# Fewer transposes between the products of an expert pair, another split of the work between engines, and another placing of the shared blocks in a gated attention and mixture-of-experts layer

## What is computed

```python
n = layernorm(x)
q, k, v = n @ W_q, ctx @ W_k, ctx @ W_v             # 8 heads of 64
attn = softmax(where(mask, q @ k.T / 8, -max))      # 1024 x 154 per head and sequence
x = x + tanh(g_xattn) * (attn @ v @ W_o + b_o)
n = layernorm(x)
scores = sigmoid(n @ gate_w.T)                      # 32 experts in 8 groups
idx = top 6 of (scores + e_bias) in the best 4 groups
w = scores[idx] / sum(scores[idx]) * 2.5
moe = sum over the 6 of w * (relu(n @ up[e].T) ** 2 @ down[e].T)       # inner width 128
shared = relu(n @ shared_up.T) ** 2 @ shared_down.T                    # inner width 512
x = x + tanh(g_ffn) * (moe + shared)
```

## Time and profile before

| | us |
|---|---|
| median of 3 runs | 822.31 (818.47 to 823.46) |
| profiled execution | 824.46 |
| its span, first to last instruction | 822.7 |
| TensorE busy in the span | 757.1 |
| GpSimd busy | 502.9 |
| VectorE busy | 447.8 |
| ScalarE busy | 389.8 |
| mean granted clock of TensorE | 0.981 |

### The profile page before, as it was taken

The page is one execution under the profiler, slowest core; times in us unless marked ns, Lnnn a source line. Parts: engine busy times, 40 slices in busy tenths (PEclk is TensorE's granted clock), DMA queues, the critical chain, the costliest instruction groups (busy, mean ns, idle before and its releaser), DMA issues.

```text
span 822.7 us, 17866 instructions
## 1 busy us (share of the span) xinstructions
PE 757.1 (92%) x5833; PEld 639.1 (78%) x5833; DVE 447.8 (54%) x1591; ACT 389.8 (47%) x1141; POOL 502.9 (61%) x471
## 2 busy tenths in 40 slices
PE   3998989999999999979999999999999999999954
PEld 2986878888888888866656678889999887888943
DVE  0426445667666666663562124444444587766775
ACT  1126555565666665652542325555545554454520
POOL 2803221248787878787777715767767777776760
PEclk9999999999999999999999999999999999999986
DMA  8900000015221212342838446666667999999988
GB/s 284 346 10 1 1 2 1 2 37 181 76 90 71 91 71 91 115 147 100 316 115 292 149 126 180 200 207 196 206 202 218 313 370 363 332 327 298 314 303 293
DMA packets 77612, 144.72 MB, mean 176 GB/s; under 512 B 12625, under 2 KB 58961, under 8 KB 77009
## 3 DMA queue, kind: packets, MB, share of 16 engines
q1 hardware_dynamic: 51936, 63.89, 25.5%
q0 software_dynamic: 19968, 56.52, 18.3%
q10 hardware_dynamic: 5616, 23.16, 8.4%
HBM read 73.80 MB, written 69.73 MB: 174 GB/s over the span
## 4 chain that ended last, share of the span: by engine, by line
PE 61%; POOL 15%; ACT 8%; issue 6%; DMA 4%; DVE 4%; DVEq 1%; POOLq 0%; SPq 0%
POOL token_parts L409 15%; PE ps L1086 7%; PE ps L982 6%; PE ps L1138 6%; PE ps L1265 5%; PE ps L1029 5%; PE ps L1150 5%; PE ps L1282 5%; PE ps L1064 4%; PE ps L1001 4%; ACT att L460 3%; PE ps L1251 3%; ACT att L469 2%; PE ps L1076 2%; DMA token_parts<-hid,place 2%
## 5 line engine op out<-in xcount | busy, mean ns | idle before, releaser
L409 POOL DMA_INDIRECT token_parts<-hid,place x224 | 223.2, 996 | 99.1 <-issue 64.3
L392 POOL DMA_INDIRECT routed_rows<-x_n,slots x120 | 117.0, 975 | 34.3 <-issue 34.3
L1265 PE MATMUL ps<-big,att 128*128 x896 | 121.5, 279 | 3.9 <-issue 2.6
L1265 PEld LDWEIGHTS ps<-big,att 128*128 128x128 f32 x896 | 110.2, 193 | 10.3 <-issue 9.7
L1282 PE MATMUL ps<-big,att 128*128 x448 | 115.7, 381 | 0.6 <-ACT att L552 0.6
L548 ACT ACTIVATE att<-ps 128x512 f32<-128x512 f32 x112 | 66.9, 597 | 90.1 <-PE ps L1251 90.1
L385 POOL TENSOR_TENSOR att<-att,rsum 128x1232 f32<-128x1232 f32 x22 | 49.4, 2245 | 87.8 <-DVE rsum L666 87.6
L469 ACT ACTIVATE att<-ps 128x512 f32<-128x512 f32 (+1 forms) x96 | 47.0, 525 | 115.9 <-PE ps L1064 115.9
L1282 PEld LDWEIGHTS ps<-big,att 128*128 128x128 f32 x448 | 76.8, 192 | 6.6 <-issue 0.8
L911 DVE TENSOR_SCALAR att<-ps 128x256 f32<-128x256 f32 x112 | 47.6, 425 | 58.5 <-PE ps L1265 55.1
L552 ACT ACTIVATE att<-ps 128x256 f32<-128x256 f32 x112 | 42.9, 383 | 62.6 <-PE ps L1273 62.6
(11 more groups left out here) (221 smaller groups left out, 1333.5 us busy)
## 6 DMA issues: line engine op xcount, KB each, us to landing
mid<-routed_rows SPq DMA_DIRECT2D x224, 138.0 KB
big<-token_parts ACTq DMA_DIRECT2D x19, 768.0 KB, 7.1
x_n<-token_parts ACTq DMA_DIRECT2D x9, 768.0 KB
routed_rows<-pad_row SPq DMA_DIRECT2D x1, 4416.0 KB, 21.3
routed_rows<-pad_row SPq DMA_DIRECT2D x32, 138.0 KB, 2.9
big<-in_x SPq DMA_DIRECT2D x4, 1024.0 KB, 14.6
big<-in_w_moe SPq DMA_DIRECT2D x2, 2048.0 KB, 8.9
big<-in_w_moe SPq DMA_DIRECT2D x1, 4096.0 KB, 13.8
```

What stands on the lines that cost most here:

```text
L392: nc.gpsimd.indirect_dma_start(rows, bass.IndirectOffsetOnAxis(ap=slots[:, t, k:k + 1], axis=0), normed(t), None).then_inc(s_sca[t // TB % ...
L409: nc.gpsimd.indirect_dma_start(parts, bass.IndirectOffsetOnAxis(ap=place[:, p // 2 % 4, p % 2 * 2 + j:p % 2 * 2 + j + 1], axis=0), y_sb[:, ...
L1265: ins = M(ps[:, 2 + p % 2, j * P:(j + 1) * P], xt[:, p % 2, j * 256 + c * P:j * 256 + (c + 1) * P], w_exp[:, bass.ds(e, 1), c * P:(c + 1) ...
```

## The change

There are six parts.

- **Pairs on TensorE.** `expert_up` has the weights as the stationary operand and the transposed rows as the moving one, so its output is already transposed and `hidden_t` is gone. The weights are copied ahead of that, by ScalarE, from the register-addressed place to one of two fixed buffers (`copy_up`). VectorE makes relu and square in two instructions (`relu_square`). `rows_t` runs two pairs ahead instead of one.
- **Output buffers.** `y_sb` has eight buffers instead of four.
- **Scaling.** Of the tiles T = 11 to 31 those with T % 4 equal to 3 or 0 (eleven) are scaled by VectorE, behind the maxima of the next tile. GpSimd sends six scatters in each iteration from T = 12 on.
- **Shared blocks.** `GAP` is 5. Blocks 5 and 6 are done between the pairs, in 16 steps at pairs 4, 10, ..., 94, and block 7 behind the last pair. The first two blocks' `down` is cut in halves around the router's products of the last block.
- **Nine token groups** instead of four, ending at tiles 4, 8, 12, 16, 20, 24, 28, 30 and 32. The table has 288 rows in three pieces, and its products are 2 columns wide where only one is used. A group's number of pairs `DONE` is 3t + 16 for an end at tile t.
- **Parts.** Tiles 0 to 23 are loaded one in three pairs from pair 32 on (32, 35, 38, 41, 44, ... 101), tiles 24 to 27 at 104, 106, 108 and 110. Of the last four, 28 and 29 wait only for the pairs of the group that ends at tile 30.

```diff
-GAP = 7
-NSEG = 4
+GAP = 5
+DVE_NORM = tuple(t for t in range(11, NT) if t % 4 in (3, 0))
-SEG_END = (12, 20, 28, NT)
+SEG_END = (4, 8, 12, 16, 20, 24, 28, 30, NT)
+PART_LOAD = {DONE[g] + 4 + 3 * i: 4 * g + i for g in range(6) for i in range(4)}
+PART_LOAD.update({DONE[6] + 4 + 2 * i: 24 + i for i in range(4)})
-SHARED_STEP = {2 + 6 * i: i for i in range(8 * (NBLK - GAP))}
+SHARED_STEP = {4 + 6 * i: i for i in range(8 * (NBLK - 1 - GAP))}
...
@@ gpsimd
                 if T >= 12:
-                    for i in range(sent, sent + 5 + T % 2):
+                    for i in range(sent, sent + TOPK):
                         scatter(i)
-                    sent += 5 + T % 2
-                normalise(T)
+                    sent += TOPK
+                if T not in DVE_NORM:
+                    normalise(T)
...
@@ scalar
-            def square(p):
-                act.wait_ge(s_ehp, p + 1)
-                A.activation(h_t[:, p % 2, :], ps[:, 2 + p % 2, 256:512], ACT.Square).then_inc(s_eht, 1)
+            def copy_up(p):
+                if p == 0:
+                    act.wait_ge(s_row, 1)
+                    for i in range(3):
+                        act.wait_ge(s_we[i], 16)
+                if p % 2 == 0:
+                    act.load(regs[p // 2 % 2], exp_i[0:1, 2 * p:2 * p + 4])
+                for j in range(2):
+                    e = act.snap(regs[p // 2 % 2][p % 2 * 2 + j], min_val=0, max_val=NE - 1)
+                    ins = A.activation(w_up[p % 2][:, j, :], w_exp[:, bass.ds(e, 1), 0:256].rearrange("p a n -> p (a n)"), ACT.Copy)
+                ins.then_inc(s_ewu, 1)
...
@@ vector
+            def normalise(T):
+                p3 = prob[T % 3][:, 0:HJ].rearrange("p (h j) -> p h j", h=NH)
+                V.tensor_tensor(p3, p3, rsum[:, T % 2, :].unsqueeze(2).broadcast_to([P, NH, J]), ALU.mult).then_inc(s_pnv, 1)
...
                     for q in range(3):
                         maxima(T, q)
+                if T - 1 in DVE_NORM:
+                    dve.drain()
+                    normalise(T - 1)
...
-                        dve.wait_ge(s_ys[p % 4], 32 * ((p - 8) // 4 + 1))
+                        dve.wait_ge(s_ys[p % 8], 32 * (p // 8))
...
-            def relu(p):
+            def relu_square(p):
                 dve.wait_ge(s_eup, p + 1)
-                V.tensor_scalar(h_tok[:, p % 2, :], ps[:, 2 + p % 2, 0:256], 0.0, None, ALU.max).then_inc(s_ere, 1)
+                h, r = ps[:, 2 + p % 2, 0:256], relu[p % 2]
+                V.tensor_scalar(r, h, 0.0, None, ALU.max)
+                dve.drain()
+                V.scalar_tensor_tensor(h_t[:, p % 2, :], h, 0.0, r, ALU.max, ALU.mult).then_inc(s_eht, 1)
...
@@ tensor
             def expert_up(p):
+                pe.wait_ge(s_xts, p + 1)
+                pe.wait_ge(s_ewu, p + 1)
+                for j in range(2):
+                    for c in range(KC):
+                        ins = M(ps[:, 2 + p % 2, j * P:(j + 1) * P], w_up[p % 2][:, j, c * P:(c + 1) * P],
+                                xt[:, p % 2, j * 256 + c * P:j * 256 + (c + 1) * P],
+                                start=c == 0, stop=c == KC - 1, skip_group_check=True)
+                ins.then_inc(s_eup, 1)
...
-                if p + 1 < N_PAIRS:
-                    rows_t(p + 1)
+                if p + 2 < N_PAIRS:
+                    rows_t(p + 2)
                 if p >= 1:
                     expert_down(p - 1)
-                if p < N_PAIRS:
-                    hidden_t(p)
```

261 lines of the change are left out of this document (153 added, 108 removed).

## The result

The changed kernel took 788.75 us (median of 4 runs, 786.80 to 789.22), the kernel before 821.36 (median of 4, 818.47 to 823.46) on the same chip: ratio 0.9596, 95% interval 0.9565 to 0.9628. The forecast was 788, range 774 to 806. Medians and ranges, here and in the experiments, are over all executions of a kernel, while ratios leave out the ones over 1.5% above its fastest. The changed kernel's profiled execution has a span of 787.4 us against 822.7.

What follows compares the result with a forecast made beforehand. TensorE was taken to bound attention, shared blocks and the pairs up to 617 us, then GpSimd's scatters, held up by VectorE's additions. Start 474 + pairs 293 + tail 21 = 788 us, range 774 to 806.

Steps and rivals of the forecast that it cites:

- Start of the pairs: First scatter of expert outputs at 474 us instead of 497, bounds 470 and 482; routed scatters end 16 us earlier.
- TensorE free at 462 to 464: Before the pairs, TensorE is done with shared blocks at 462 to 464 us instead of 489.1, slot wait included.
- The scaling on VectorE: In attention, eleven products of 1.44 us delay the residual by 0 to 7.5, taken under 1; lock 1, bound 12.
- Pace: Pairs: 2.53 us without parts, 2.65 with them (GpSimd 2.63, VectorE 2.62 overlapping); 293 from first to last scatter.
- Weight copies on ScalarE: In the pairs, two copies a pair at 0.40 us each, bounds 0.32 and 0.63; 0.42 a pair more, hidden.
- Tail: From last scatter to end of span: 21.1 us instead of 24.6, bounds 18 and 24.6.
- Two sums instead of four: At the end, two of the four last tiles are summed before the last scatter lands: 3.5 us less.
- Block 7 hidden: Behind the last pair, some 17 us of shared block begin up to 15 ahead of the last scatter, costing nothing.
- rival 2: Better cover: pairs at 2.57 us and a warm TensorE in the tail, 779 us; chance 10%.
- (1): In the pairs, engines too near one another wait for each other: 2.80 us a pair with parts, 800 us; chance 22%.
- (3): The pairs' early start fails, block 7's slots or the table being late: +16, 804 us; chance 9%.
- (4): VectorE falls behind in the pairs, TensorE idles and drops to 1.2 GHz: 843 us with 30 such pairs; chance 5%.

Runs made afterwards that it cites:

- run 128*128: Not a follow-up run: in a profile row of the changed kernel, `run` is a buffer read by a TensorE product, followed by its shape; no time of its own.
- the second group: Four kernels on a chip like the result's: the changed kernel unaltered, 788.19 us (ratio 0.9602 to the kernel before), and three edits of it.
- the run with reductions: Against the changed kernel, a tile's six parts are added by two one-input reductions and one two-input addition on VectorE: 811.02 us against 788.19.

## Why the prediction was right, and where its steps were not

*Start of the pairs, 474 forecast, 476.3 found.* The count of scatters stood: row 30's scaling last, 78 scatters behind it, no wait for slots but one of 0.33. The 2.9 us of the difference (459.7 to 462.6) are these: row 30's scaling ended at 363.5 and the 78 scatters began at 363.7 instead of 361.4, 2.3 us late, of which the 0.9 that the working had set aside for block 6's slots wasn't needed, so 1.4; and 1.5 us went into longer ones among them (one of 1.59, one of 1.31, some of 1.05). The 3.0 us to the first load (3.2), 3.3 to the rows (3.0) and 7.5 to 8 to the first scatter (7.45) were met. What I gave as the cause was the whole package; the runs divide it: 11.6 us by six scatters in every iteration (a count from two traces; the run that takes back this edit alone was disturbed), 1.8 by the scaling. And this gain could only come because two blocks had left the front: with seven, the start is TensorE's.

*TensorE free at 462 to 464* was wrong, it was 468.5. It stood 3.05 us for block 7's slots, as the working had allowed, but then ran at less than full clock (granted 0.50 from 427 to 432 us, 1.00 from 434 on):

```profile
427.04 0.41 PE L1273 MATMUL ps<-ones_bf,run 128*128 128x2 bf16 x6 [3.05 <-DVE att L851]
...
427.43 6.39 PE L1187 MATMUL ps<-mid,w_shared 128*128 128x512 f32 x8
```

Eight instructions in 6.39 us, where the earlier trace rows have 16 in 6.87. This cost nothing, since the rows landed at 468.9, and was even of use: it left no gap. Had TensorE been free at 463 as forecast, it would have stood almost 6 us ahead of the rows. The experiment with all scalings on GpSimd shows what a gap of 3.58 us does there, 3.2 us more; the working priced the wait for the rows and not the clock behind it.

*The scaling on VectorE: under 1 us of cost, lock included.* The scaling took the 1.44 us that the working gave it. It lengthened the scatters by 0.77 us each, hidden; my bound of 1.1 was too low for a single one (the longest was 1.2 longer). As a whole the edit was a gain of 5.3 us. The step that failed is the one that looked only for its cost: I let its use be part of the 16 us, without asking what the last 2 us at the meeting point are worth. The Trainium skill (SBUF — State Buffer, section SBUF: two separate sides) describes a lock that fits this, between a VectorE instruction with two SBUF inputs and a GpSimd operation that reads SBUF. The traces agree where VectorE is first: long scatters behind the beginning of additions with two SBUF inputs, none beside reductions with one, none where the additions are left out. The same section has the engine that begins first hold up the other for its whole instruction, and for a scatter that is first the traces show otherwise: 20 additions began inside a running scatter of the changed kernel and took at most 0.97 us, like the rest.

*Pace, 2.53 and 2.65 forecast, 2.54 and 2.66 found; stretch 293 and 293.0.* The term for the scatters was right in kind, and since GpSimd waits for next to nothing but its issue, floor and excess must add up to the pace: 2.53 + 10.6 / 79.5 = 2.663 is the pace behind pair 32 to the third figure, and in the second group 2.53 + 9.3 / 79.5 = 2.647 and 2.53 + 11.5 / 79.5 = 2.675 give the measured 2.647 and 2.674. Its size was 8 and became 10.6; a part of that is a slip, for 28 tiles at 0.33 are 9.2 and not 8. VectorE's 2.62 a pair was given equal weight as a cause; it was too high (about 2.49 by the run with reductions) and caused nothing (GpSimd waited 1.5 us for it in 280) until the reductions made it longer, and then it showed at once. So the second of the two terms that overlap at 2.65 failed, and the first carried the number. Taking the transposes off TensorE was worth 11.2 us in time, the largest part of those taken back alone on the undisturbed chip. The stretch before was longer by only 8.1; that it had fewer late shared steps than with GAP 5 would explain this, and no run tests it.

*Weight copies on ScalarE, 0.40 and hidden.* 0.409 us each, and TensorE waited for them 0.7 us in all:

```profile
L1324 PE MATMUL ps<-att 128*128 128x128 f32 x896 | 118.1, 275 | 0.7 <-ACT att L570 0.7
L570 ACT ACTIVATE att<-big 128x256 f32 x224 | 80.2, 409 | 1.3 <-issue 0.9
```

*Tail, 21.1 forecast, 18.05 found.* Two steps failed, and the measured time lies at the lower bound of the range given. "Two sums instead of four" is false: the loads of tiles 28 and 29 were issued early, but TensorE works in the order of its program, and all four sums stand behind block 7. "Block 7 hidden" is false as well: it began 6.9 us ahead of the start of the last scatter and not 15, and from 762.45 to the end TensorE is the chain; the last tile's parts, loaded at about 773 and there some 6 us later, come while it works. Against the kernel before, 3.2 us of the 6.5 are the warm clock, 6.92 us for four sums instead of 10.1, which the working held only as its bound of 18 and in rival 2; the other 3.3 are that the sums begin 8.5 us behind the last scatter where the working kept 11.8.

*The sum.* 476.3 + 293.0 + 18.05 = 787.4. The start was 2.3 late and the tail 3.05 short: the nearness of 788 to 788.75 is in part these two against each other, and so in part luck. (The working says 34.7 us less of span and takes 34.3 off the median; the 0.4 is rounding.)

*The rivals.* (1), pace 2.80 by engines too near each other, did not come: GpSimd hardly waited. Whether the eight buffers are the reason is open. (2) was half right, by the warm tail, wrong by the pace. (3) did not come in this kernel, though TensorE did wait for block 7's slots. (4) did not come; the experiment with the reductions shows VectorE behind, and there TensorE stood 15 us for it in the 180 of the window, never over 0.8 at once, and the granted clock stayed at 1.00, so doubled products are not what a VectorE that is late in this way brings.

## What to carry to other kernels

When an engine's wait has only its own issue as releaser, it is the bound, and its pace can be computed: its floor plus the excess of its long instructions. Look then for what is late next before giving any neighbour more work: here VectorE had about 0.16 us a pair of room (an estimate from the run with reductions), 6% of the pace, and 1.2 us more a tile cost 23 us, over twice what the long scatters had cost. Where two paths meet, ask for each edit which of them it shortens: the same edit can be worth nothing, its own length, or its length plus a spell of slow clock, depending on which side of the meeting the other path stands.
